# LSTM z and gate weights as scaled f16 pairs in place of rounded f32 pairs

## Time and profile before

| | |
|---|---|
| median of 3 timed runs (lowest to highest) | 658.39 us (657.45 to 660.18) |
| the profiled execution's own time | 654.01 us |
| its span, first to last instruction | 652.2 us |
| mean granted clock of PE | 0.973 |
| busy: PE, PEld | 599.0 us (92%), 379.7 us (58%) |
| busy: DVE, ACT, POOL | 510.1 us (78%), 470.0 us (72%), 391.8 us (60%) |

### The profile page before, as it was taken

One profiled execution on the slowest core, in us unless ns is written; L12 is line 12 of the kernel. 1 busy time (PEld: TensorE's weight loads), 2 busy tenths in 40 slices (PEclk: granted clock), 3 DMA queues, 4 the chain that ended last, 5 costly groups with the idle time before them and its releaser, 6 DMA issues.

```text
span 652.2 us, 14360 instructions
## 1 busy us (share of the span) xinstructions
PE 599.0 (92%) x4968; PEld 379.7 (58%) x4968; DVE 510.1 (78%) x1204; ACT 470.0 (72%) x838; POOL 391.8 (60%) x385
## 2 busy tenths in 40 slices
PE   1899899899999999999999999955999999999996
PEld 0344344578888888888888888842333343333332
DVE  4789875399999999999999999996667667657432
ACT  2589778799999999999999999965344344344320
POOL 1478948355555555555555555568667677667670
PEclk9899989899999999999999999985999999999999
DMA  9978920004442244443234444007798998999996
GB/s 236 273 233 266 219 29 1 10 4 65 66 62 35 37 66 65 66 66 50 33 49 65 66 65 65 3 1 205 212 264 265 279 276 263 262 260 276 266 268 183
DMA packets 96424, 89.30 MB, mean 137 GB/s; under 512 B 78240, under 2 KB 79520, under 8 KB 96288
## 3 DMA queue, kind: packets, MB, share of 16 engines
q1 hardware_dynamic: 89536, 70.00, 46.6%
q10 hardware_dynamic: 6816, 18.38, 9.9%
HBM read 35.07 MB, written 16.78 MB: 79 GB/s over the span
## 4 chain that ended last, share of the span: by engine, by line
PE 67%; SPq 14%; DVE 8%; DMA 5%; ACT 3%; issue 2%; POOL 1%; ACTq 1%; DVEq 0%; POOLq 0%
PE ps L1160 18%; PE ps L1138 12%; PE ps L1214 9%; PE ps L1165 9%; SPq L406 8%; PE ps L1142 6%; SPq L412 5%; PE ps L1083 5%; PE ps L1084 4%; DMA shifted<-pad 4%; PE ps L1204 2%; DVE bn L473 2%; DMA ident<-in_consts_dram 1%; ACT xn L895 1%; POOL lo L800 1%
## 5 line engine op out<-in xcount | busy, mean ns | idle before, releaser
L819 POOL TENSOR_TENSOR fc<-gate,cell 128x352 f32<-128x352 f32 (+16 forms) x96 | 83.8, 873 | 144.6 <-ACT gate L969 144.6
L850 POOL COPY shifted<-pad 32x1073 f32<-32x1073 f32 x128 | 137.5, 1074 | 54.8 <-DVE pad L733 48.4
L1160 PE MATMUL ps<-z_hi,wg_hi 128*128 128x352 f32 (+13 forms) x384 | 134.2, 351 | 2.9 <-ACT z_hi L953 2.9
L1160 PE MATMUL ps<-z_hi,wg_lo 128*128 128x352 f32 (+13 forms) x384 | 122.5, 321 | 0.0
L1214 PE MATMUL ps<-shifted,wt_hi 128*32 128x512 f16 x1536 | 108.5, 389 | 8.5 <-DMA shifted<-pad 8.5
L1165 PE MATMUL ps<-z_lo,wg_hi 128*128 128x352 f32 (+13 forms) x384 | 107.6, 321 | 0.0
L969 ACT ACTIVATE gate<-ps,gate_bias 128x352 f32<-128x352 f32 (+16 forms) x192 | 104.2, 543 | 1.6 <-PE ps L1165 1.4
L740 DVE SCALAR_TENSOR_TENSOR img<-ps,y_unscale,img 128x512 f32<-128x512 f32 x64 | 47.8, 747 | 69.4 <-PE ps L1214 69.4
L969 ACT ACTIVATE ps<-ps,gate_bias 128x352 f32<-128x352 f32 (+16 forms) x192 | 99.5, 518 | 0.2 <-PE ps L1165 0.2
L1004 ACT ACTIVATE pad<-img,nbias,rstd 128x1024 f16<-128x1024 f32 x32 | 39.8, 1244 | 80.4 <-PE ps L1214 71.9
L829 POOL TENSOR_TENSOR img<-hT,xr 128x352 f32<-128x352 f32 (+1 forms) x96 | 88.7, 924 | 1.7 <-DVE hT L695 1.7
(11 more groups left out here) (121 smaller groups left out, 1116.4 us busy)
## 6 DMA issues: line engine op xcount, KB each, us to landing
shifted<-pad SPq DMA_DIRECT2D x128, 134.1 KB, 4.0
shifted<-pad ACTq DMA_DIRECT2D x128, 134.1 KB, 4.1
xr<-in_x_dram SPq DMA_DIRECT2D x64, 256.0 KB, 5.6
img<-in_x_dram SPq DMA_DIRECT2D x126, 128.0 KB, 3.5
out_dram<-img SPq DMA_DIRECT2D x60, 256.0 KB, 4.5
shifted<-shifted SPq DMA_DIRECT2D x2, 553.5 KB, 6.0
out_dram<-img SPq DMA_DIRECT2D x16, 64.0 KB, 1.9
raw_c<-in_L_conv_W_dram SPq DMA_DIRECT2D x4, 144.0 KB, 2.7
```

Source lines behind the costliest of these rows:

```text
L819: pool.tensor_tensor(fc[it % 2][:, 0:c1 - c0], gate[it % 2][0][:, 0:c1 - c0], cell[:, c0:c1], ALU.mult).then_inc(fc_done, 1)
L850: pool.tensor_copy(shifted[b % SLOTS][32:64, q, ROWS_AT:ROWS_END].bitcast(F32), pad[b % SLOTS][32 * q:32 * q + 32, ROWS_AT:ROWS_END].bitca ...
L1160: pe.matmul(gbank(it, m)[:, 0:n], w[:, GATE_ORDER[m], :], z_hi[it % 2][:, 0:n], start=(w is wg_hi), stop=False)
```

## The change

z and the gate weights become f16 pairs.

- `z_hi` and `z_lo` are f16. The scale on z is the constant `Z_HALF` = 1 / (64 x 512), an immediate, in `high_z` and in `zlow`; what is left of z's scale, a power of two, stays in z.
- The gate weights are multiplied by that power of two and by one of their own, so that the largest comes near 4096, and split into f16. The activation of each gate undoes it: besides the bias pointer it gets a scale pointer, `gate_unscale`.
- The gate weights' largest value has to be found over all partitions. At image 16 DVE (`peak_gates`) copies `wgT`, reduces the 512 columns, multiplies by `z_unscale` and spreads the result over 128 columns; PE transposes that at image 18; at image 19 DVE (`scale_gates`) reduces 128 columns and runs `scale_of`. The split moves from image 16 to image 22 and gets a multiplication ahead of it.
- `even_width`, `offset` and `z_even` go; all widths are exact. `prep_T` counts one more transpose, so the waits on it rise by one. A filler tile keeps `xr` where it was.

```diff
+Z_HALF = 1.0 / (Z_TOP * ACT_SCALE)
+PEAK_AT, TURN_PEAK_AT, PEAK_SCALE_AT, SPLIT_GATES_AT = 16, 18, 19, 22
-            wg_hi = sb("wg_hi", [P, GATES, P], F32R, s01)
-            wg_lo = sb("wg_lo", [P, GATES, P], F32R, s01)
+            wg_hi = sb("wg_hi", [P, GATES, P], F16, s01)
+            wg_lo = sb("wg_lo", [P, GATES, P], F16, s01)
-                z_hi = [sb(f"z_hi{i}", [P, WIDEST], F32R, s1) for i in range(2)]
-                z_lo = [sb(f"z_lo{i}", [P, WIDEST], F32R, s1) for i in range(2)]
+                z_hi = [sb(f"z_hi{i}", [P, WIDEST], F16, s1) for i in range(2)]
+                z_lo = [sb(f"z_lo{i}", [P, WIDEST], F16, s1) for i in range(2)]
+                sb("between", [P, 640], F32, s1)
...
-            def split_gates():
+            def peak_gates():
 
                 v.wait_ge(prep_T, 3)
                 v.tensor_copy(wgT[:], wgroup(2)).then_inc(wgt_done, 1)
-                split(2, wg_hi, wg_lo)
+                step(v.tensor_reduce(top[:, 2:3], wgroup(2), AX.XY, ALU.max, apply_absolute_value=True))
+                settle()
+                step(v.tensor_scalar(top[:, 3:4], top[:, 2:3], z_unscale[:], None, ALU.mult))
+                settle()
+                v.tensor_scalar(peaks[:], ident[:], 0.0, top[:, 3:4], ALU.mult, ALU.add).then_inc(peaks_done, 1)
+
+            def scale_gates():
+
+                v.wait_ge(prep_T, 4)
+                step(v.tensor_reduce(peak[:, 2:3], wgroup(2)[:, 0], AX.X, ALU.max))
+                scale_of(2, WEIGHT_TOP, 1.0 / WEIGHT_TOP, gate_unscale, gate_scale_ready)
+                v.wait_ge(gate_scale_ready, 1)
+                step(v.tensor_scalar(top[:, 2:3], scl[:, 8:9], z_unscale[:], None, ALU.mult))
+
+            def split_gates():
+
+                settle()
+                v.wait_ge(wgt_done, 1)
+                v.tensor_scalar(wgroup(2), wgT[:], top[:, 2:3], None, ALU.mult).then_inc(wgs_done, 1)
+                v.wait_ge(wgs_done, 1)
+                v.tensor_copy(wg_hi[:], wgroup(2)).then_inc(prep_hi, 1)
+                v.wait_ge(prep_hi, 3)
+                v.tensor_tensor(wg_lo[:], wgroup(2), wg_hi[:], ALU.subtract).then_inc(split_done, 1)
...
-                v.scalar_tensor_tensor(out=z_lo[it % 2][:, 0:n], in0=z_even(it), scalar=z_unscale[:],
-                                       in1=z_hi[it % 2][:, 0:n].bitcast(F32), op0=ALU.mult,
+                v.scalar_tensor_tensor(out=z_lo[it % 2][:, 0:n], in0=z_of(it), scalar=Z_HALF,
+                                       in1=z_hi[it % 2][:, 0:n], op0=ALU.mult,
...
-                act.activation(z_hi[it % 2][:, 0:even_width(it)], z_even(it), ACT.Identity,
-                               scale=z_unscale[:]).then_inc(z_hi_done, 1)
+                act.activation(z_hi[it % 2][:, 0:width(it)], z_of(it), ACT.Identity,
+                               scale=Z_HALF).then_inc(z_hi_done, 1)
...
-                               bias=gate_bias[:, gt:gt + 1]).then_inc(gate_done, 1)
+                               bias=gate_bias[:, gt:gt + 1], scale=gate_unscale[:]).then_inc(gate_done, 1)
...
+                if b == TURN_PEAK_AT:
+                    pe.wait_ge(peaks_done, 1)
+                    turn(2, lambda k: peaks[:], 1)
```

More of the change, by code:

```diff
@@ L9 @@
 F32 = mybir.dt.float32
-F32R = mybir.dt.float32r
 F16 = mybir.dt.float16
@@ L88, in width @@
     return c1 - c0
[L91 to L98, removed]
 PADW = W + 1
@@ L132, in build_network @@
         z_unscale = sb("z_unscale", [P, 1], F32)
+        gate_unscale = sb("gate_unscale", [P, 1], F32)
         y_unscale = sb("y_unscale", [P, 1], F32)
@@ L146, in build_network @@
         bsum = sb("bsum", [P, 1 + GATES], F32)
-        top = sb("top", [P, 8], F32)
-        scl = sb("scl", [P, 6], F32)
+        top = sb("top", [P, 4], F32)
+        peak = sb("peak", [P, 3], F32)
+        clip = sb("clip", [P, 3], F32)
+        scl = sb("scl", [P, 9], F32)
         rstd = [sb(f"rstd{i}", [P, CH], F32) for i in range(2)]
@@ L168, in build_network @@
             mask = sb("mask", [P, P], F32, s01)
+            peaks = sb("peaks", [P, P], F32, s01)
             with ExitStack() as s0:
@@ L214, in build_network @@
         wgt_done = sem("wgt_done")
+        peaks_done = sem("peaks_done")
+        gate_scale_ready = sem("gate_scale_ready")
+        wgs_done = sem("wgs_done")
         prep_hi = sem("prep_hi")
@@ L276, in z_of @@
             return zbank(it)[:, at:at + width(it)]
-        def z_even(it):
-            at = columns(it)[0] - W * TOUCHED[it % NB][0] - offset(it)
-            return zbank(it)[:, at:at + even_width(it)]
         def gate_columns(it, m):
-            return gbank(it, m)[:, offset(it):offset(it) + width(it)]
+            return gbank(it, m)[:, 0:width(it)]
         def gbank(it, n):
@@ L581, in split @@
                 v.wait_ge(prep_hi, n + 1)
-                high = hi[:].bitcast(F32) if n == 2 else hi[:]
-                v.tensor_tensor(lo[:], wgroup(n), high, ALU.subtract).then_inc(split_done, 1)
-            def split_gates():
+                v.tensor_tensor(lo[:], wgroup(n), hi[:], ALU.subtract).then_inc(split_done, 1)
+            def peak_gates():
                 v.wait_ge(prep_T, 3)
                 v.tensor_copy(wgT[:], wgroup(2)).then_inc(wgt_done, 1)
-                split(2, wg_hi, wg_lo)
+                step(v.tensor_reduce(top[:, 2:3], wgroup(2), AX.XY, ALU.max, apply_absolute_value=True))
[17 more added lines that the diff above has]
+                v.tensor_tensor(wg_lo[:], wgroup(2), wg_hi[:], ALU.subtract).then_inc(split_done, 1)
             def split_conv(d):
-                v.wait_ge(prep_T, 4 + d)
+                v.wait_ge(prep_T, 5 + d)
                 v.wait_ge(wall_hi_done, d + 1)
@@ L643, in _ @@
                     scale_weights()
-                if b == TURN_GATES + EVAC_LAG:
+                if b == PEAK_AT:
+                    peak_gates()
+                if b == PEAK_SCALE_AT:
+                    scale_gates()
+                if b == SPLIT_GATES_AT:
                     split_gates()
@@ L650, in zlow @@
             def zlow(it):
-                n = even_width(it)
+                n = width(it)
                 v.wait_ge(z_hi_done, it + 1)
-                v.scalar_tensor_tensor(out=z_lo[it % 2][:, 0:n], in0=z_even(it), scalar=z_unscale[:],
-                                       in1=z_hi[it % 2][:, 0:n].bitcast(F32), op0=ALU.mult,
+                v.scalar_tensor_tensor(out=z_lo[it % 2][:, 0:n], in0=z_of(it), scalar=Z_HALF,
+                                       in1=z_hi[it % 2][:, 0:n], op0=ALU.mult,
                                        op1=ALU.subtract).then_inc(z_lo_done, 1)
@@ L805, in _ @@
                                        ALU.add).then_inc(bias_summed, 1)
-            pool.wait_ge(prep_T, 3 + 3)
+            pool.wait_ge(prep_T, 4 + 3)
             pool.memset(cell[:], 0.0).then_inc(c_done, NB)
@@ L913, in high_conv @@
             def high_conv(d):
-                act.wait_ge(prep_T, 4 + d)
+                act.wait_ge(prep_T, 5 + d)
                 act.activation(wall_hi[:, d], wconv_ps, ACT.Copy).then_inc(wall_hi_done, 1)
@@ L928, in _ @@
             act.wait_ge(z_scale_ready, 1)
-            turn(turn_i, raw_i, 2, scl[:, 4:5])
+            turn(turn_i, raw_i, 2, scl[:, 6:7])
             for b in range(B):
@@ L936, in _ @@
                 if b == 0:
-                    act.activation(raw_s[:], raw_s[:], ACT.Identity, scale=scl[:, 4:5]).then_inc(raws_ready, 1)
+                    act.activation(raw_s[:], raw_s[:], ACT.Identity, scale=scl[:, 6:7]).then_inc(raws_ready, 1)
                 if b == TURN_CONV_AT:
                     act.wait_ge(scales_ready, 1)
-                    turn(turn_c, raw_c, 9, scl[:, 5:6])
+                    turn(turn_c, raw_c, 9, scl[:, 7:8])
                 if b == B - 1:
```

22 lines of the change are left out of this document (11 added, 11 removed).

## The result

The change makes the kernel slower by 0.65%: 660.21 us against 655.92, medians of 20 runs each (655.32 to 665.09 and 652.15 to 660.46), ratio 1.0065, 95% interval 1.0042 to 1.0088. That is +4.3 us where +6.6 were forecast from the first three runs of before, whose median of 658.39 was itself 2.5 too high.

The account below looks back on a forecast made before the run. PE was taken to bound the LSTM at 3.209 us an item, with ACT taking over at 3.27: +5.8 us there and +0.8 in the first stage, +6.6 on 658.4, gave 665.0 us, range 656 to 673.

Parts of the forecast that it names:

- The sign and the mechanism: LSTM stage: slower, because four gate pointers make ACT take over from PE, at 3.27 us an item against 3.209.
- With 0.09 each: 3.629 - 7 x 0.09 = 3.00: LSTM, ACT's need per item before the change: seven durations summed, less an overlap of 0.09 each, gives 3.00 us.
- the term of +5.8: LSTM stage: ACT at 3.27 an item instead of 3.209, over 95 items, adds 5.8 us.
- Rival 2: LSTM: the two cancel, ACT ends at 3.18 to 3.22 an item, total 656 to 661 us; chance 0.13.
- Rival 1: LSTM: the second pointer is hidden, PE's f16 pace sets 3.07 an item, total 645 to 655 us; chance 0.14.
- rival 3: LSTM: ACT is dearer than the sum, 3.41 an item, total 671 to 678 us; chance 0.13.
- the formula's 3.40: LSTM, ACT per item by the Trainium skill's instruction costs: 3.12 before and 3.40 after, 18 us slower.
- tanh has 0.2 to spare: LSTM, walk of one item at 3.27 us: cell ends at 2.65, ACT's tanh starts at 2.87.
- First stage, +0.8: First stage: new DVE work delays turn_c by about 1.2, partly hidden at PE's image 22; +0.8 us, bounds -2.5 to +3.3.
- Gates at 633 and 608 ns, z_hi 455: LSTM, expected ACT durations as signs: gates up from 543 and 518 ns, z_hi near 455.
- under 0.50 apart: LSTM, a falsifier: the forecast is wrong if gates follow one another in under 0.50 us.
- The first z_hi moves by more than 3 us: Start of the LSTM, a falsifier: the forecast is wrong if the first z_hi shifts by more than 3 us.

Follow-up runs that it names:

- gate_immediate: The changed kernel with the gates' scale as an immediate constant 2^-15 instead of the pointer, output scale not right: 644.47 us, ratio 0.985 to before, 3.070 an item.
- no_gate_scale_search: The changed kernel without the gate weights' scale search and multiplication, split unscaled at image 16, scale pointer a column of ones: 656.96 us, ratio 1.0021 to before.
- gate_pointer_alone: The kernel before with a scale pointer, a column of ones, added to the four gate activations, f32r kept: 664.33 us, ratio 1.0141, 3.315 an item.
- broadcast_from_psum: The changed kernel with the peaks broadcast's input read from PSUM instead of SBUF: 658.66 us, ratio 1.0063 to before.

## Why the prediction was right and wrong

- *The sign and the mechanism* held. f16 gates bring PE to 3.07 (gate_immediate), the pointers' net cost on ACT is 4 x 0.092 - 0.093 = 0.275, where 0.27 was forecast, ACT takes over and is full, and no other engine holds the item. But the LSTM adds only 0.6 to 1.0 us to the loss, and with the search taken out (no_gate_scale_search, 1.0021, 0.999 to 1.0051) the total isn't told from before's: that the kernel is measurably slower is due to the first stage, not to the term that the forecast rested on.
- *"With 0.09 each: 3.629 - 7 x 0.09 = 3.00"* is the step that failed. ACT's own need was 2.95 at most (3.315 - 4 x 0.092). The overlap was (3.629 - 2.95) / 7 = 0.097 or more, not the 0.09 taken from five pairs read to 0.01 us, and it isn't the same for all kinds (load's was 0.07, z_hi's 0.12). Seven times 0.007 is 0.05 an item, 5 us over 95: the term of +5.8 measured +0.6 to +1.0. The difference of two large sums (3.27 - 3.209) was put at two digits where its error was as large as itself. The distances from start to start, which need no durations, would have given it: 2.92 in the trace of before.
- *Rival 2*, the two cancel, is what the LSTM did (3.22, its upper edge), by the second of the reasons that it named, overlaps of 0.10; the first, a pointer at 0.06, is out. The prediction gave it 0.13. *Rival 1*, hidden pointers, is excluded by gate_pointer_alone; *rival 3* and the formula's 3.40 by 3.215.
- *"tanh has 0.2 to spare"* was right at 3.27, but the walk didn't close the ring cell, tanh, hrow, cell; that ring is near 3.1, and it decides once ACT and PE are quicker.
- *First stage, +0.8*: measured +2.8. The steps at image 19 cost 1.27 (87.04 to 88.31 on DVE) as forecast. The broadcast was put at 0.3 by its columns and took 2.03 because of POOL: 1.7 of the missing 2.0. What is left, +1.1 where 0.8 was forecast, is what was to be hidden at PE's image 22. Nothing was: turn_c and the first z_hi are later by the same amount (+1.1 both in broadcast_from_psum). In the kernel before, image 22's matmuls already waited for POOL's lo, which comes behind ACT's hi, so there was nothing to hide it in:

```profile
93.92 0.10 PEld L1083 LDWEIGHTS ps<-lo,wi_hi 128*128 128x128 f16 x1 [0.45 <-POOL lo L800]
```

- *That the total came within 2.3 us of the forecast change* (+4.3 against +6.6) is in part luck: the LSTM's term was 5 too high and the first stage's 2 too low.
- *Gates at 633 and 608 ns, z_hi 455*: wrong as signs (725, 702, 545), see below. The falsifier "under 0.50 apart" was the sound one: 0.52. "The first z_hi moves by more than 3 us" came about (3.5 in the profiled executions, 2.8 counted from image 16).
- *The carried-over median* of before was 658.39 from three runs; 20 runs gave 655.92. The change of 6.6 was set on a base 2.5 too high. *0.13 x 95*, for f16 alone, is 12, not 13; with the 0.14 an item that it comes to, 13 is right.

## What to carry to other kernels

A narrower operand type speeds up the engine that multiplies, but count what undoes its scale: here one scale pointer on an activation cost 0.09 us of ACT each time, and it was cheapest where there were fewest instructions, ahead of the product instead of behind it. Before an engine is called idle enough, measure start-to-start distances of pairs in which nothing waits, and follow every ring of dependences once round. Where a DVE operation over many columns goes from SBUF to SBUF beside a busy POOL, as the broadcast did, look whether it waits for POOL, and take its input from PSUM if it is there.

## What the runs showed of the hardware that was not expected

An ACT instruction's recorded duration is longer where ACT has had no gap for a while, with no change in its distances; over the LSTM of the changed kernel it rises and falls. The first gate of the LSTM, one in the middle, and one behind a gap of 0.28 us, all of the changed kernel:

```profile
129.18 0.64 ACT L988 ACTIVATE gate<-ps,gate_bias,gate_unscale 128x351 f32<-128x351 f32 x1
...
199.58 0.71 ACT L988 ACTIVATE gate<-ps,gate_bias,gate_unscale 128x352 f32<-128x352 f32 x1
...
431.45 0.64 ACT L988 ACTIVATE gate<-ps,gate_bias,gate_unscale 128x352 f32<-128x352 f32 x1 [0.28 <-PE ps L1187]
```

0.64 and 0.64 beside 0.71 for the same 351 to 352 columns (and 0.76 at 310.85 above, with only 339). In gate_immediate, where ACT has small waits all along, the one-pointer gates are at 0.53 to 0.54 in mid-stage. Durations of a full ACT therefore can't be summed to its need, and longer durations of untouched instructions were here a sign that it had become the bound. Why the record grows was not tried.
